# Layer normalisation in the output stage: variance by a Square pass on ScalarE, the normalising pass one turn later

## What is computed

```python
def _layernorm(x, axis=-1, eps=1e-05):
    m = jnp.mean(x, axis=axis, keepdims=True)
    v = jnp.var(x, axis=axis, keepdims=True)
    return (x - m) / jnp.sqrt(v + eps)
```

## Time and profile before

| | us |
|---|---|
| median of three runs | 4287.79 (4287.08 to 4290.51) |
| profiled execution, device time | 4294.91 |
| its span | 4293.2 |
| output stage, plain stretch used here | 3780 to 4260, 90 tiles |
| mean granted TensorE clock over the span | 0.92 |

### The profile page before, as it was taken

How to read it: one execution, slowest core, us unless ns; L and a number is a source line. 1 busy time by engine, 2 the same in 40 slices (tenths; PEclk the granted TensorE clock), 3 DMA queues, 4 the chain that set the end, 5 groups by cost and what they waited for, 6 DMA issues and landing times. The chain is left out here.

```text
span 4293.2 us, 67317 instructions
## 1 busy us (share of the span) xinstructions
PE 3523.8 (82%) x21804; PEld 2146.3 (50%) x21805; DVE 2163.2 (50%) x5213; ACT 1302.1 (30%) x2233; POOL 1009.2 (24%) x1392
## 2 busy tenths in 40 slices
PE   4850039999999999999999999999999930188898
PEld 3640025566555655565556555655565520055565
DVE  8877254434443444334434443344334300389998
ACT  2531113322332233223322332233223300044444
POOL 2448710000000000000000000000000037466665
PEclk9985559999999999999999999999999975599999
DMA  8862011111111111111121111111111000278887
GB/s 256 256 211 61 3 38 40 44 56 34 48 40 56 37 46 37 57 38 45 38 56 38 46 40 53 39 48 38 53 39 48 29 13 1 49 213 231 231 230 211
DMA packets 147427, 337.78 MB, mean 79 GB/s; under 512 B 81880, under 2 KB 81880, under 8 KB 139738
## 3 DMA queue, kind: packets, MB, share of 16 engines
q1 hardware_dynamic: 111883, 240.88, 18.4%
q0 software_dynamic: 34112, 93.04, 8.5%
q10 hardware_dynamic: 1175, 0.05, 0.0%
HBM read 266.09 MB, written 124.25 MB: 91 GB/s over the span
## 5 line engine op out<-in xcount | busy, mean ns | idle before, releaser
L942 POOL DMA_INDIRECT lay_rows<-parts,lay_idx x200 | 210.1, 1051 | 2536.2 <-PE lay_pz L1185 1619.2
L1219 PE MATMUL lay_pm<-lay_zh,w1h 128*128 128x500 f16 x1920 | 718.4, 374 | 25.3 <-DVE lay_h L1105 20.1
L1220 PE MATMUL lay_pm<-lay_zl,w1h 128*128 128x500 f16 x1920 | 718.6, 374 | 1.8 <-issue 1.3
L1221 PE MATMUL lay_pm<-lay_zh,w1l 128*128 128x500 f16 x1920 | 718.4, 374 | 0.0
L1026 DVE SCALAR_TENSOR_TENSOR lay_zl<-lay_pz,lay_zh 128x400 f16<-128x400 f32 x600 | 320.4, 574 | 710.7 <-ACT lay_zh L1136 710.5
L1136 ACT ACTIVATE lay_zh<-lay_pz 128x400 f16<-128x400 f32 x600 | 298.3, 504 | 1056.9 <-PE lay_pz L1185 1053.2
L1145 ACT ACTIVATE lay_ex<-lay_pm,b1c,scale 128x500 f32<-128x500 f32 x320 | 245.6, 768 | 869.8 <-PE lay_pm L1221 869.8
L1243 PE MATMUL lay_pm<-w2h,lay_gh 128*128 128x512 f16 x1280 | 484.9, 379 | 0.0
L1243 PE MATMUL lay_pm<-w2h,lay_gl 128*128 128x512 f16 x1280 | 483.9, 378 | 0.0
L1243 PE MATMUL lay_pm<-w2l,lay_gh 128*128 128x512 f16 x1280 | 483.4, 378 | 0.0
L1061 DVE TENSOR_SCALAR lay_ex<-lay_ex,scale 128x500 f32<-128x500 f32 x320 | 153.7, 480 | 568.0 <-ACT lay_ex L1145 568.0
(11 more groups left out here) (278 smaller groups left out, 5775.1 us busy)
## 6 DMA issues: line engine op xcount, KB each, us to landing
x<-in_x_dram SPq DMA_DIRECT2D x20, 1500.0 KB
out_x<-x SPq DMA_DIRECT2D x100, 288.0 KB
out_own<-h SPq DMA_DIRECT2D x100, 288.0 KB
out_dram<-out_x SPq DMA_DIRECT2D x100, 288.0 KB
nrm_xb<-in_x_dram SPq DMA_DIRECT2D x20, 1344.0 KB
parts<-nrm_parts SPq DMA_DIRECT2D x20, 1344.0 KB
h<-lay_h SPq DMA_DIRECT2D x80, 336.0 KB
nrm_w<-in_L_gnn_W_dram SPq DMA_DIRECT2D x6, 1024.0 KB, 19.3
```

Source lines behind the costliest of these rows:

```text
L1219: pe.matmul(o, c.w1h[:, d, cols], zh[:, d, h], start=(d == 0), stop=False)
L1220: pe.matmul(o, c.w1h[:, d, cols], zl[:, d, h], start=False, stop=False)
L1221: ins = pe.matmul(o, c.w1l[:, d, cols], zh[:, d, h], start=False, stop=(d == DC - 1))
```

## The change

DVE no longer takes statistics. Its addition L1635 becomes a scalar_tensor_tensor that also sums each row, and two small instructions give the negated mean (`nm`) and the same divided by the root of 768 (`nms`). ACT begins its turn with a Square pass over x of tile t that subtracts the mean and sums the squares, which gives the variance (`spread2`). POOL's chain gets one more link in front, which adds epsilon. The normalising pass stays last in ACT's turn but now works on tile t-1. All that follows it moves one turn later: the transposes and the copy work on tile t-2, the hidden step on tile t-3, gelu and the second matmul on tile t-4, the last addition and the output on tile t-5. The last turn is 104. The x loads stay at tile t+4, and x keeps its ten slots.

```diff
-        FIRST, LAST = -AHEAD, TILES + 3
+        FIRST, LAST = -AHEAD, TILES + 4
...
-                t, at, there, ok = tile_at(grp, j, -4)
+                t, at, there, ok = tile_at(grp, j, -5)
                 if ok:
                     sp.wait_ge(o_ready, t + 1)
                     for lo, hi in row_parts(OT):
...
-                    nw = Chain(pool, newton, 6 * t)
-                    pool.wait_ge(ve_ready, t + 1)
+                    nw = Chain(pool, newton, 7 * t)
+                    pool.wait_ge(dev_ready, t + 1)
+                    nw.link(nc.gpsimd.tensor_tensor(ve_, spread2[:, at % 2:at % 2 + 1], eps[:], ALU.add))
...
-                    nc.vector.tensor_tensor(x[:, at], x[:, at], pa[0:OT, 0:D], ALU.add).then_inc(x2_ready, 1)
-                    dve.wait_ge(x2_ready, t + 1)
-                    for half in range(2):
-                        lc.put(nc.vector.bn_stats(stats[:, b, half], x[:, at, half * (D // 2):(half + 1) * (D // 2)]))
-                    lc.wait()
-                    nc.vector.memset(spare[:], 0.0)
-                    lc.link(nc.vector.bn_aggr(mv[:, b], stats[:, b].rearrange("p a b -> p (a b)")))
                     if beyond(t, 2):
                         dve.wait_ge(norm_ready, t - 1)
-                    nc.vector.tensor_scalar(nm[:, col], mv[:, b, 0:1], -1.0, None, ALU.mult)
-                    nc.vector.tensor_scalar(ve[:, col], mv[:, b, 1:2], EPS, None, ALU.add).then_inc(ve_ready, 1)
+                    nc.vector.scalar_tensor_tensor(out=x[:, at], in0=x[:, at], scalar=1.0, in1=pa[0:OT, 0:D], op0=ALU.mult,
+                                                   op1=ALU.add, accum_out=total[:, col]).then_inc(x2_ready, 1)
+                    dve.wait_ge(x2_ready, t + 1)
+                    nc.vector.tensor_scalar(nms[:, col], total[:, col], -1.0 / D ** 1.5, None, ALU.mult)
+                    nc.vector.tensor_scalar(nm[:, col], total[:, col], -1.0 / D, None, ALU.mult).then_inc(mean_ready, 1)
...
-                tf, af, _, okf = tile_at(grp, j, -4)
+                tf, af, _, okf = tile_at(grp, j, -5)
...
             def iteration(grp, j):
+                t, at, _, ok = tile_at(grp, j, 0)
+                if ok:
+                    act.wait_ge(mean_ready, t + 1)
+                    if beyond(t, 1):
+                        act.wait_ge(dev_ready, t)
+                    if beyond(t, 2):
+                        act.wait_ge(norm_ready, t - 1)
+                    b = at % 2
+                    nc.scalar.activation(dev[:], x[:, at], ACT.Square, bias=nms[:, b:b + 1], scale=D ** -0.5,
+                                         accum_out=spread2[:, b:b + 1]).then_inc(dev_ready, 1)
...
-                t, at, _, ok = tile_at(grp, j, 0)
+                t, at, _, ok = tile_at(grp, j, -1)
                 if ok:
                     act.wait_ge(norm_ready, t + 1)
```

More of the change, by code:

```diff
@@ L1394, in stage_output @@
         att = m.sb("att", [OE, AB, OT])
-        stats, mv = m.sb("stats", [OT, 2, 2, 6]), m.sb("mv", [OT, 2, 2])
+        dev, total, spread2 = m.sb("dev", [OT, D]), m.sb("total", [OT, 2]), m.sb("spread2", [OT, 2])
+        nms, eps = m.sb("nms", [OT, 2]), m.sb("eps", [OT, 1])
         ve, nm, rough, sq, rstd, shift = (m.sb(n, [OT, 2]) for n in ("ve", "nm", "rough", "sq", "rstd", "shift"))
@@ L1406, in stage_output @@
         sems = ("par_in", "turned_w", "w_ready", "init", "posed", "slots_in", "idx_ready", "mask_ready",
-                "looked", "weights_ready", "att_ready", "agg_done", "x2_ready", "ve_ready", "norm_ready", "newton", "xn_ready",
+                "looked", "weights_ready", "att_ready", "agg_done", "x2_ready", "mean_ready", "dev_ready", "norm_ready", "newton", "xn_ready",
                 "turned", "xt_ready", "h_done", "u_ready", "t_ready", "th_ready", "g_ready", "o_done", "o_ready",
@@ L1410, in stage_output @@
         (par_in, turned_w, w_ready, init, posed, slots_in, idx_ready, mask_ready, looked, weights_ready,
-         att_ready, agg_done, x2_ready, ve_ready, norm_ready, newton, xn_ready, turned, xt_ready, h_done, u_ready, t_ready,
+         att_ready, agg_done, x2_ready, mean_ready, dev_ready, norm_ready, newton, xn_ready, turned, xt_ready, h_done, u_ready, t_ready,
          th_ready, g_ready, o_done, o_ready, own_added, chain, setup, gelu, prep, bias_in, held, paused) = (
@@ L1512, in _ @@
             nc.gpsimd.memset(onehalf[:], 1.5).then_inc(posed, 1)
+            nc.gpsimd.memset(eps[:], EPS).then_inc(posed, 1)
             nc.gpsimd.memset(rows[:], 0.0).then_inc(posed, 1)
-            pool.wait_ge(posed, 4)
+            pool.wait_ge(posed, 5)
             def iteration(grp, j):
@@ L1580, in _ @@
             ch.wait()
-            nc.vector.memset(stats[:], 0.0).then_inc(w_ready, 1)
+            nc.vector.memset(total[:], 0.0).then_inc(w_ready, 1)
             def slot_math(grp):
@@ L1629, in iteration @@
                 col = slice(b, b + 1)
-                lc = Chain(dve, chain, 3 * t)
+                lc = Chain(dve, chain, t)
                 if ok:
@@ L1634, in iteration @@
                     dve.wait_ge(own_added, t + 1)
-                    nc.vector.tensor_tensor(x[:, at], x[:, at], pa[0:OT, 0:D], ALU.add).then_inc(x2_ready, 1)
-                    dve.wait_ge(x2_ready, t + 1)
-                    for half in range(2):
-                        lc.put(nc.vector.bn_stats(stats[:, b, half], x[:, at, half * (D // 2):(half + 1) * (D // 2)]))
-                    lc.wait()
-                    nc.vector.memset(spare[:], 0.0)
-                    lc.link(nc.vector.bn_aggr(mv[:, b], stats[:, b].rearrange("p a b -> p (a b)")))
                     if beyond(t, 2):
                         dve.wait_ge(norm_ready, t - 1)
-                    nc.vector.tensor_scalar(nm[:, col], mv[:, b, 0:1], -1.0, None, ALU.mult)
-                    nc.vector.tensor_scalar(ve[:, col], mv[:, b, 1:2], EPS, None, ALU.add).then_inc(ve_ready, 1)
-                    assert lc.n == 3, lc.n
+                    nc.vector.scalar_tensor_tensor(out=x[:, at], in0=x[:, at], scalar=1.0, in1=pa[0:OT, 0:D], op0=ALU.mult,
[3 more added lines that the diff above has]
+                    nc.vector.tensor_scalar(nm[:, col], total[:, col], -1.0 / D, None, ALU.mult).then_inc(mean_ready, 1)
                 if next_group(grp):
@@ L1662, in iteration @@
                     rows_now(grp + 1, 1)
-                tg, ag, _, okg = tile_at(grp, j, -3)
+                tg, ag, _, okg = tile_at(grp, j, -4)
                 gb = ag % 2
@@ L1697, in iteration @@
                     nc.scalar.activation(th[:, ag % 2], u2[:, ag % 2], ACT.Tanh, scale=GELU_C).then_inc(th_ready, 1)
-                t, at, _, ok = tile_at(grp, j, -1)
+                t, at, _, ok = tile_at(grp, j, -2)
                 if ok:
@@ L1705, in iteration @@
                         .then_inc(xt_ready, 1)
-                th_, ah_, _, okh = tile_at(grp, j, -2)
+                th_, ah_, _, okh = tile_at(grp, j, -3)
                 if okh:
@@ L1764, in iteration @@
                     ins.then_inc(turned, 1)
-                t, at, _, ok = tile_at(grp, j, -2)
+                t, at, _, ok = tile_at(grp, j, -3)
                 if ok:
@@ L1772, in iteration @@
                     ins.then_inc(h_done, 1)
-                t, at, _, ok = tile_at(grp, j, -3)
+                t, at, _, ok = tile_at(grp, j, -4)
                 if ok:
```

## The result

The changed kernel takes 4446.72 us (median of four runs, 4437.1 to 4457.7); the kernel before, run beside it, 4289.15. The ratio is 1.0369, 95% interval 1.0352 to 1.0386. It is slower, as forecast, and by more: 158 us against the 120 predicted. The profiled execution took 4457.69 us, 11 us above the median, with a span of 4455.9.

A forecast was written before the change was run, and what follows sets the result against it. VectorE bounds most turns now; after the change, SyncE's waits for landings would. Loop +105.7, turns before +6, after +11.2, fill and drain -3: together +120, 4415 on the profiled execution, forecast 4408 us; range 4310 to 4470.

The forecast's parts named there:

- The step that decides: SyncE's queue: each x load waits for the landing of the output issued just before; loop groups 68.8 us against 53.7.
- L in a plain turn: SyncE's queue, turns without record loads: time from an output's issue to the x load behind it, taken as 3.6 us.
- seven groups of the loop: Output stage's loop, ten tiles per group: each group +15.1 us, +105.7 in all.
- sixteen turns after it: Output stage after the loop: 88.2 us against 77.0 today, +11.2.
- fill and drain: One more pipeline turn (0 to +5 us) and VectorE's saving in turns SP doesn't bind (0 to -11): -3.
- The landing behind record loads: SyncE's queue, three turns of ten: output's issue to the next x load, 2.7 us alone, taken as 3.6.
- The gather's part: Output's landing: a gather of 0.39 MB beside it adds up to 1.3 us; 3.6 taken between 2.7 and 4.0.
- The lower bound: SyncE's queue: the program's last output, running alone, puts output issue to next x load at at least 2.2 us.
- Cost on the path: 0: ScalarE: the added pass over 768 elements fits into idle time before Tanh and makes nothing behind it later.
- the ring: SyncE's queue: output, landing, x, own, records, output, for every tile from 10 to 99; 32.8 us issuing plus ten landings per group.
- The first: Rival: outputs land in under 2.09 us, GpSimd's chain binds and the change gains, about 4241 us; chance 7%.
- The fourth: Rival: pauses drop TensorE's granted clock to 1.2 of 2.4 GHz and it passes SyncE's turn, about 4480 us; chance 10%.

The follow-up runs named there:

- old_ahead5: The kernel before with one constant changed, x loaded five tiles ahead instead of four: 4434.95 us, ratio 1.0336 to the kernel before.
- new_res: The changed kernel with its last addition written to a buffer of its own, from which the output goes: 4333.51 us, ratio 1.0092 to the kernel before.
- new_no_gather: The changed kernel with only the first ten gathers of message rows, so it leaves work out: 4408.99 us, ratio 1.0262 to the kernel before.
- new_g3: The changed kernel with the gather one turn earlier, the wait for the landing left in: 4451.91 us, ratio 1.0358 to the kernel before.
- old_deep_res: The kernel before, old statistics, later stages one turn later, output from a buffer of its own: 4298.86 us, ratio 1.0011 to the kernel before.
- old_deep: The kernel before, old statistics kept, only the later stages moved one turn later: 4459.98 us, ratio 1.0385 to the kernel before.
- new_x_last: The changed kernel with SyncE issuing own and records before x in each turn: 4327.58 us, ratio 1.0071 to the kernel before.

## Why the prediction was right, and where it was short

**The step that decides held.** The prediction put the loss into the wait of the x load for the output issued just before it, for every tile from 10 to 99, 90 waits and over 150 us; there were 90 and 295 us. The one-constant experiment (old_ahead5) and its opposite (new_res) show it from both sides. SyncE's waits for VectorE didn't go altogether: ten are left, 39.7 us, and all but 0.2 us of them stand at the start and end of the stage. VectorE's share fell to 54%, the DMA share to 59%, 6 points below what was expected.

**The mis-sized term was L in a plain turn.** By the output issues at the ends of each part of the stage, and by the two profiled executions' spans of 4293.2 and 4455.9 us, the terms of the sum compare so:

| term | predicted | measured |
|---|---|---|
| seven groups of the loop | +105.7 | +142.1 (518.3 against 376.1) |
| four turns before it | +6 | +7.7 |
| sixteen turns after it | +11.2 | +21.2 |
| fill and drain | -3 | -2.1 |
| stages ahead of the output stage | 0 | -6.2 |
| sum | +120 | +162.7 |

Issuing was put at 32.8 us per group and measured 31.4 in the group shown. The landing behind record loads was put at 3.6 and measured 3.5 over the stage; without a gather, 2.7 and 2.9. The landing in a plain turn was put at 3.6 and measured 4.5, and seven of them in each group carry the whole shortfall. The gather's part was put at 0.9 and measured 0.6. So the part that was too small is the landing without a gather, put at 2.7 and measured 3.9. Of its three pieces the start, put at 0.8, and the receipt, put at 0.9, measured 0.7 and 0.6 in the turn shown. The step that failed is "The three are 0.92 MB; at the 295 GB/s of a stretch with the engines 97% busy that is 3.1 us": in that turn they took 4.5 us, 205 GB/s on average. The rate itself was that of SyncE's queue (no other queue of data moved a packet from 3929 to 3930 in the kernel before), but in a stretch in which transfer followed transfer. In the new order the queue runs empty at every landing, so each turn pays for a slow start and a slow end, and only the middle comes near 295. Why the first 0.9 us are slow stays open.

**The lower bound was useful.** 2.2 us from the last output alone was enough to fix the sign, since 2.09 was break-even, and no L in the rows shown fell below 2.8. The prediction's estimate from the Trainium skill, "DMA: Bandwidth & Descriptors", section "Anatomy of one DMA", was 2.7 us for an output alone. That section gives its fit for transfers that GpSimd starts, and SyncE starts the output; new_no_gather's 2.8 behind record loads comes out close to it all the same. The section "Queues, rings and completion order" of that page of the Trainium skill says that on each DMA engine descriptors are consumed in ring order; that the landing without a gather grows by 1.1 us, from 2.8 to 3.9, when x and `own` stand right ahead fits it.

**The costs by engine.** ScalarE's pass is 0.93 us and its accumulator read 0.19, longer than the 0.1 put as a bound; together 1.12 where about 1.1 was allowed. VectorE's new addition costs 0.945 us, the old one 0.946, so the 0.07 us for another form were not needed, and its accumulator read is 79 ns. GpSimd's link is 0.24. These were sound. "Cost on the path: 0" for ScalarE was not, as it turned out: true in the changed kernel, where the ring covers it (new_g3), but 35 us in new_res, set against old_deep_res. The working asked whether anything behind the new wait becomes later and did not ask what the Square pass itself stands behind, and who waits for it: GpSimd's chain, the gather behind that, and TensorE.

**The rivals.** The first, that outputs land in time and the change gains, was priced at 4241 us with GpSimd as the next bound. Without the ring the kernel takes 4333, so that price was 92 us too low; it left out the second ring. With that out too it is 4275. The fourth, TensorE's clock: it did fall over the stage, from 0.96 to 0.88, and to between 0.86 and 0.91 in every kernel that has the whole ring (old_ahead5, old_deep, new_g3, new_no_gather), while it is 0.97 in new_x_last. No run has the whole ring without the fall. But from 3780 to 4406 us SyncE's queue, which sets the turn, waited only 0.2 us for VectorE, and so for anything that TensorE delivers; a slower TensorE is not in the ring there. TensorE itself still spends 172 us waiting for VectorE. Whether its clock costs anything at the two ends of the stage is not shown.

## What to carry to other kernels

When a pipeline gets one turn deeper, count the slots of every buffer that lives through it: a store that was issued a turn ahead of the wait for its landing may now stand directly before it, in the same in-order queue, and every load behind it pays the full landing. A separate buffer for what is stored, or other transfers issued between the store and the wait, takes this away. And a pass moved to an idle engine must be checked in both directions: what it delays, and what the queue in front of it delays on its side, through every engine that waits for its result.

## What the runs showed of the hardware

A 300 KB output took 2.8 us from its issue until the next instruction that waited for it, where no gather ran and SyncE's queue had moved nothing for the last 0.4 us (new_no_gather at 4008.45); 3.9 on average with x and `own` just ahead; 4.5 with the gather too, and up to 5.6 in the rows shown. x, `own` and an output, 0.92 MB issued one behind the other on SyncE's queue with no other traffic, took 4.5 us to move: 0.9 us at 106 GB/s, 2.7 at 273 and 0.9 at 99 (new_no_gather from 3974.70). The accumulator read is an instruction of its own on both engines, 0.19 us on ScalarE and 0.08 on VectorE. The scalar_tensor_tensor form with one PSUM operand took 0.945 us, as long as the plain addition with one PSUM operand in the kernel before, 0.946; the same form with both operands in SBUF 1.01.
